# Selecting the rows of B with all 128 rows of the array instead of 64, in a fused state-space, attention and mixture kernel

## What is computed

```python
x = L0_attn_x
x = x + 0.5 * _L0_ffn_ref(_layernorm(x), w_gate, w_up, w_down)
x = x + _L0_attn_ref(_layernorm(x), ...)
x = x + 0.5 * _L0_ffn_ref(_layernorm(x), w_gate, w_up, w_down)
x = x + 0.5 * _L1_ffn_ref(_layernorm(x), Wg, bg, W1, b1, W2, b2)
x = x + _L1_attn_ref(_layernorm(x), Wq, Wk, Wv, Wo, rel, gamma, beta)
x = x + 0.5 * _L1_ffn_ref(_layernorm(x), Wg, bg, W1, b1, W2, b2)
```

```python
deltaA = jnp.exp(delta[..., None] * A)
deltaBx = delta[..., None] * Bm[:, :, None, :] * u[..., None]
h = dA * h + dBx
y = jnp.einsum('ben,n->be', h, c)
```

## Time and profile before

| what | value |
|---|---|
| median of three executions | 2872.73 us |
| time of the profiled execution | 2876.84 us |
| its span, first to last instruction | 2875.1 us |
| TensorE (PE) busy | 2733.4 us, 95% |
| weight loads (PEld) busy | 1895.2 us |
| VectorE (DVE) busy | 1946.4 us, 68% |
| ScalarE (ACT) busy | 1606.0 us, 56% |
| GpSimd (POOL) busy | 1371.3 us, 48% |
| mean granted clock of TensorE | 0.953 of 2.4 GHz |

### The profile page before, as it was taken

The page is one execution under the profiler, slowest core; times in us unless marked ns, Lnnn a source line. Parts: engine busy times, 40 slices in busy tenths (PEclk is TensorE's granted clock), DMA queues, the critical chain, the costliest instruction groups (busy, mean ns, idle before and its releaser), DMA issues.

```text
span 2875.1 us, 41563 instructions
## 1 busy us (share of the span) xinstructions
PE 2733.4 (95%) x14913; PEld 1895.2 (66%) x14913; DVE 1946.4 (68%) x3753; ACT 1606.0 (56%) x3405; POOL 1371.3 (48%) x1226
## 2 busy tenths in 40 slices
PE   7999999999999989999799899999999999999888
PEld 7777875786577655666366566656575666678675
DVE  5868887697868687676867886687858666432320
ACT  2433436435664556656486556756675676465654
POOL 2448475563737365454716474274636635311111
PEclk9999999999999989799799999999999999999899
DMA  4223122131213021211202121121202112000000
GB/s 147 67 67 104 55 64 74 45 92 42 79 40 96 23 73 39 70 49 49 77 20 78 37 76 31 49 70 31 75 19 86 36 52 67 1 4 1 1 5 4
DMA packets 88573, 150.60 MB, mean 52 GB/s; under 512 B 10565, under 2 KB 21485, under 8 KB 88110
## 3 DMA queue, kind: packets, MB, share of 16 engines
q1 hardware_dynamic: 88366, 147.94, 16.4%
HBM read 145.26 MB, written 2.65 MB: 51 GB/s over the span
## 4 chain that ended last, share of the span: by engine, by line
PE 83%; ACT 7%; DVE 5%; POOL 3%; issue 2%; DMA 0%; POOLq 0%; SPq 0%; ACTq 0%; DVEq 0%
PE c_bank L912 16%; PE c_bank L920 16%; PE c_bank L1338 13%; PE a_bank L758 8%; PE a_bank L748 5%; PE b_bank L1072 3%; PE b_bank L1061 3%; PE a_bank L727 2%; PE b_bank L1085 2%; PE b_bank L1084 2%; PE b_bank L582 1%; PE b_bank L563 1%; PE b_bank L565 1%; PE b_bank L1083 1%; PE a_bank L764 1%
## 5 line engine op out<-in xcount | busy, mean ns | idle before, releaser
L829 POOL TENSOR_TENSOR prod_c<-hst,prod_c 128x512 f32<-128x512 f32 x512 | 666.0, 1306 | 502.0 <-DVE hst L706 478.1
L706 DVE TENSOR_TENSOR_SCAN hst<-dA,a_bank 128x512 f32<-128x512 f32 x512 | 621.0, 1213 | 16.3 <-ACT dA L818 6.8
L912 PE MATMUL c_bank<-c_xT,w 128*128 128x512 f32 x1024 | 544.3, 638 | 7.7 <-ACT weighted_y L955 4.7
L818 ACT ACTIVATE dA<-delta,a_neg 128x510 f32<-128x510 f32 x512 | 364.2, 718 | 330.8 <-DVE hst L706 325.4
L920 PEld LDWEIGHTS c_bank<-w,hid 128*128 128x128 f32 x4096 | 491.2, 193 | 80.0 <-issue 47.5
L920 PE MATMUL c_bank<-w,hid 128*128 128x128 f32 x4096 | 529.4, 281 | 3.1 <-ACT hid L947 3.1
L1338 PEld LDWEIGHTS c_bank<-ident 128*128 128x128 f32 x3752 | 449.1, 193 | 66.4 <-issue 60.4
L1338 PE MATMUL c_bank<-ident 128*128 128x128 f32 x3752 | 483.4, 281 | 0.5 <-ACT weighted_y L955 0.4
L947 ACT ACTIVATE hid<-c_bank,b 128x512 f32<-128x512 f32 x512 | 349.7, 687 | 185.2 <-PE c_bank L912 183.5
L700 DVE TENSOR_TENSOR a_bank<-du,a_bank 128x512 f32<-128x512 f32 x512 | 350.5, 685 | 132.7 <-PE a_bank L748 128.5
L971 POOL TENSOR_TENSOR xs<-xs,weighted_y 128x512 f32<-128x512 f32 x128 | 167.9, 1312 | 544.6 <-ACT weighted_y L955 544.0
(11 more groups left out here) (179 smaller groups left out, 3550.8 us busy)
## 6 DMA issues: line engine op xcount, KB each, us to landing
prod_c<-c_rows SPq DMA_DIRECT2D x512, 256.0 KB, 3.1
w<-in_w SPq DMA_DIRECT2D x2, 2048.0 KB
xs<-in_x SPq DMA_DIRECT2D x8, 256.0 KB, 8.6
bias<-skew SPq DMA_DIRECT2D x1, 2048.0 KB, 8.8
out_dram<-xs SPq DMA_DIRECT2D x8, 256.0 KB, 2.3
in_wT<-in_in_wT SPq DMA_DIRECT2D x1, 512.0 KB
c_rows<-bcC SPq DMA_DIRECT2D x16, 32.0 KB, 1.6
b_hq<-in_w_gu SPq DMA_DIRECT2D x1, 384.0 KB, 3.2
```

The source lines that it names most:

```text
L706: nc.vector.tensor_tensor_scan(hst[:, s % RS, :], dA[:, s % RA, :], b_bank, 0.0, ALU.mult, ALU.add).then_inc(M.h.sem, 1)
L818: nc.scalar.activation(half_batches(dA[:, s % RA, :], 1), half_batches(delta[:, h, :], 1), ACT.Exp, scale=a_neg[:, l, h, n:n + 1]).then_in ...
L829: nc.gpsimd.tensor_tensor(prod[:, s % RP, :], hst[:, s % RS, :], cring[:, s % RC, :], ALU.mult).then_inc(M.pp.sem, 1)
L912: nc.tensor.matmul(S.bank[up_bank(e, c)][:, :], w1[:, e, c * 128:(c + 1) * 128], S.xT[:, :], start=True, stop=True).then_inc(M.up.sem, 1)
```

## The change

`bc3` is cleared as a whole at the start, `sel` is made over all 128 partitions (`eye2` has zero rows in partitions 0 to 63), and the B step reads all 128 rows of both, so zeros are multiplied by zeros in the lower half. The sum is the same. The clearing counts on the semaphore `s_const`, so the waits on it are one higher, and VectorE's first step that writes to `bcr`, ahead of the one that writes to `bc3`, waits for it too.

```diff
@@ mamba_dve
             dve.wait_ge(M.cE.sem, L.at(M.cE, 1))
+            if l == 0 and L.g == 0:
+                dve.wait_ge(s_const, 3 + RA)
@@ mamba_pe
-                    nc.tensor.matmul(S.bank[2 - s % 2 * 2][:, :], sel[64:128, s % NST, :], bc3[64:128, :],
+                    nc.tensor.matmul(S.bank[2 - s % 2 * 2][:, :], sel[:, s % NST, :], bc3[:, :],
                                      start=True, stop=True).then_inc(M.b.sem, 1)
@@ a_pe, and the same in a_act, b_pool and c_pool
-                        pe.wait_ge(s_const, 2 + RA)
+                        pe.wait_ge(s_const, 3 + RA)
@@ a_pool
-            pool.wait_ge(s_const, 1 + RA)
+            nc.gpsimd.memset(bc3[:, :], 0.0).then_inc(s_const, 1)
+            pool.wait_ge(s_const, 2 + RA)
             pool.wait_ge(s_wm, 16 * len(load_m))
-            nc.gpsimd.tensor_copy(sel[64:128, :, :], eye2[64:128, :].unsqueeze(2).to_broadcast([64, NST, 128])).then_inc(s_const, 1)
-            yield
-            pool.wait_ge(s_const, 2 + RA)
+            nc.gpsimd.tensor_copy(sel[:, :, :], eye2[:, :].unsqueeze(2).to_broadcast([128, NST, 128])).then_inc(s_const, 1)
+            yield
+            pool.wait_ge(s_const, 3 + RA)
```

The five step orders are made anew: the same steps of each lane in the same sequence, otherwise interleaved, and 1843 filler steps in the place of 1876. One line of each ORDER_PE, from the second pass:

```diff
-    "d10adb5aba2b4a2b2a3b2dad10a2d5ad9ad10a2d9a2d3ad7ad2a2d7ad3a2d7ad3a2d7ad3a2d12ad13ad7ad20ad4a3d13ad5ad3a2d7a"
...
+    "adb5a2bad2ad4b4ab4a3d7ad7ad2a2d7ad10a2d10a2d3ad7ad2a2d7ad2a2d7ad2a2d7ad3a2d12ad13ad7ad20ad3a3d13ad5ad3a2d7a"
```

More of the change, by code:

```diff
@@ new lines @@
+    "c4b2cbc12b3d2bdbcbcb4c3bc2bc2b2c2b2c4bcb2cb2c2b2cbcb3cbcb2cb2cb2cbcb2cbcbcbcbcb3cbcb2cbcb2cbcbcb2cb2cb2cbcbc"
+    "b2cbcbcb4cbcb3cb3cb3cb3cb3cb3cb3cb3cb3cb3cb2cb2cb2cbc2bc2bc5bcb3cbcbcbc2bcb2c4bc2bc2b2cbcb3cb3cb3cb3cb3cb3c"
+    "b3cb3cb3cb3cb3cb3cb3cb3cb2cb2cbcbcbcbcb3cbcbcb2cbcbcbcb2cb3cbcb2cbcb2cbcbcb2cb3cbcb2cbcb2c2bcbcb2cbcbcbcb2"
+    "d27c68")
+ORDER_DVE = (
+    "ab70aba7b8a3baba3ba3b5ab2ababa4baba6baba2ba2ba2ba2ba2ba2ba2ba2ba8ba2bab7a135b13a7ba3bab2abab2a3bababababa2b"
+    "a2ba5ba2ba2ba2ba2ba2ba2ba2ba2ba2ba8ba2ba2ba2ba2ba2ba2ca2ca2ba2bca2ba2ba2ba2ba2ba2ba2cacb5ababcbcbcbabcbcb5ab"
+    "a5b2a4b4a14ba72b13a7ba3bab2abab2a3bababababa2ba2ba5ba2ba2ba2ba2ba2ba2ba2ba2ba2ba8ba2ba2ba2ba2ba2ba2ca2ca2ba2"
+    "bca2ba2ba2ba2ba2ba2ba2cacb4abab2cbcbabcbcbcb5aba5b2a4b4a14baba2ba2ba2ba2ba7b5a8b2aba2ba2ba2bababa2ba2ba2ba2b"
+    "a2ba2ba2ba2ba2ba2ba2ba2babab2a2b2ab2a2b6a2b2a5bab9ab2a5b2a4b3abababa11baba2ba2ba2ba2ba2ba2ba2ba2ba2ba2ba2ba2"
+    "ba2ba2ba2ba2ba2ba2ba2ba2ba2ba2ba2ba2ba2ba2ba6ba2ba3b5cbc4a2b3ab5c4a2ca8ba6ba8baba2bab5aba2ba2ba2ba2bab5aba2b"
+    "ab2a4b5cbacac3b7aba7cbaba2ca2ba2ba2babcbcbaba2ba2ba2ba2ca2ba2ba2ba2ba2ba2bab4ababab2a4bab8a6ba4b5ab2ab2ab2a3"
+    "b3ababa2ba2ba2baba2ba2ba2ba2ba2ba2bab2a2b2a2b2a2b2a2b2a2b2a2b2a2b2a2b2a2b2ab2a2b2ab2a2b2a2b3aba2b2a2b2ab2a2"
+    "b2a2b2a2b2ab2a2b2a2b2ab2a2b2a2b2a2b2a2b2c4bcb2ab8cbc3a5ca2ba2b23a13b5abacaca2ca2babababababcbcba10b2a2bababa"
+    "bcababababababa2cababa2cababababcababababababa2ca3b5aba5b4aba5b8abab3aba3b4a2b18ab2a2b2a2baba3b2ab2ab2ab2ab2"
+    "a3baba3bababab2aba2b2a2b2a2baba2b2a2b2a2baba2b2a2b2a2b2a2b2a2b2a2b2a6baba4b5abaca2ca2cababcbabababababaca6ba"
+    "ba2babababcabcbcbcb2abacb2ab10a8b5abac4acbab3ababababa8baba3babababababababababa2baba2babababababababababa7"
+    "b5aba5b4aba8b8ab4abab4acab2aca2cb2ab2aca2b2ab2a2b2cb4a2b4a5b2ab19aba2b2a3b2a2b2a2b4ab2ab2ab2ab2a3b2a2b2ab2a7"
+    "baba4b5aba2ca2cbabababababababaca2ca2ca2baba2babababababababababa3baba3babababababababababcacacaca2b5abacaca"
+    "c2bcbcb5aba2b10ababa3baba3bab5ab2ababa8b5aba5b4aba8b8abab7abab2a2b2a2b2a2b2ababababa2b2a2b2acab2acacbcba2bab"
+    "acababa2baba3b2a5b2a3b2a4b2a2b2a3b2ab4ab2ab2a5b2ab12ab2a4b2a2b2a5b2a4b2abacabaca2bcabcaca5bababab4aba7cacbcb"
+    "ca3cbabababababababababa3baba2babababababababababa6b5aba2ca2cb4abaca2ca2ca3b9a2b3ab13ab2a3b2a2b2ab2aca2c3b2a"
+    "b2ab2ab2ca3b2ab2a3b2a2b2ab2a7b2a3b2a2b3aba3b2ab2a3b2a2b2a2b2a2b2a3b2a2b2a2b2a2b2a2baba2baba11ba2ba4ba2ca2ca2"
+    "cac2a3b5c4b7cb30cbc4b13cb3cbc2b5cb69c5b10c5b86c10")
@@ new lines @@
+ORDER_POOL = (
+    "ab5a2b2a13ba86bab2a18ba12ba15ba2ca2b2aca7ca6ca6ca9ca3ca9ca3ca6bab2a18ba12ba15ba2ca2b2aca6baca3ba3ba3ca3ca6c"
+    "a5ca5ca2ca61bcabca4ca2baca5ca2ca2ba2cbcac2aba16ba12cbacabab2c3a8ca14ca8ca18cbabcbc2bcacaba2ca4cacba2ca13ba10"
+    "ba5ba4baba3ca2ca2caca7ca17ca4ba3ca2ca3baca10bab3ca7ca3baca7ca3ba2ca4ba2cba3ba3cac2a15ca4ca3ba4ca4cba5ca8ca2b"
+    "aca3c2a6ba5ba3bacbcbcabaca2baba3ca4caca4c2a24ca7ca3c3a2baca4c3ba15cba6ca3caba3ca2ba4ba3ca3bacac3a7ca6ca8ca6c"
+    "a4ca12ca5c3ab2c2bc2bc2b2cbc11b3c17")
```

127 lines of the change are left out of this document (49 added, 78 removed).

## The result

| | before | after |
|---|---|---|
| median of four executions | 2874.28 us | 2762.74 us (2759.75 to 2769.06) |
| ratio of the times, 95% interval | | 0.9607 (0.9576 to 0.9639) |
| time of the profiled execution | 2876.84 us | 2769.06 us |
| its span | 2875.1 us | 2767.3 us |

The change makes the kernel 3.9% faster. The profiled executions are 107.8 us apart; 94 us were forecast. (The median of before stood at 2872.73 us when the forecast was made; the fourth execution, run beside the kernel after, is 2885.39 us.)

A forecast was written before the change was run, and what follows sets the result against it. TensorE, 95% busy, was taken as the bound, with VectorE and GpSimd close behind in four filler passes. B steps (135 us) and fillers (7) free 142 us; 94 arrive: 2783 us profiled, 2779 median, 8-in-10 range 2728 to 2835.

The forecast's parts named there:

- The price of a B step: On TensorE between 128-row matmuls: 0.10 us into it, 0.08 to 0.09 out, 0.11 for late weights; 0.29 us in all.
- the step that carried the forecast: The B step's delay comes from its changed row height, not its bf16 type, so 128 rows save the full 0.29 us.
- What reaches the end: Of 142 us freed on TensorE, 15 in passes 0, 1, 2 and 4 and 79 elsewhere shorten the total: 94 us.
- gains of 4, 3, 4 and 4 us: Passes 0, 1, 2 and 4, full of fillers, were to shorten this much: 15 of 43 us freed on TensorE.
- the bound of the scan step: In passes 0, 1, 2 and 4 a scan step needs 1.93 us on GpSimd and 1.91 on VectorE, against 2.1 now.
- a fifth: Taken off the 99 us freed in the other passes, for chain latencies and added fillers, leaving 79 us.
- Behind the last scan: The stretch with no B step left was to stay as it is, some 430 us, with 28 more fillers.
- The additions: Clearing bc3, at most 0.52 us on GpSimd, and sel over 128 partitions, 1.9 us as before, hidden before the first B step.
- The whole gain: Rival: the new interleaving fills every hole and all 142 us arrive, 2735 us, range 2715 to 2750; 13%.
- Half the gain: Rival: the data type costs something, 0.08 to 0.2 us saved per step, or VectorE bounds dense passes; 2800 to 2855; 17%.
- no gain: Rival: the delay comes with bf16 weights, so only the 7 us of fillers go, 2866 to 2873; 5%.
- The slower case: Rival: less busy TensorE in passes 0, 1, 2 and 4 gets the lower clock, 170 to 200 us longer, 2950; 5%.

The follow-up runs named there:

- the two heights in one kernel: The kernel after with every odd B step (256 of 512) reading only partitions 64 to 127: 2821.66 us, ratio 0.981.
- a third height: The kernel after with the B step reading only 32 rows, partitions 64 to 95, leaving out the third part of B: 2864.54 us, ratio 0.9936.
- the scores with fp32 data: The kernel after with attention scores made from all 128 rows of q and k instead of a head's 24, computation changed: 2709.21 us, ratio 0.9407.
- taking away 16 pairs of changes: The kernel after with the product of gate weights and experts' second biases reading 128 rows instead of 8: 2745.23 us, again 2748.44; ratios 0.9526 and 0.9538.

## Why the prediction was right

- **The price of a B step** (0.29 us) holds to about 0.01 us at each of its three places, as the timelines of the result show, and the step that carried the forecast, that it is the height and not the type, is shown three times: by the two heights in one kernel, by a third height with the same price, and by the scores with fp32 data. Nothing of the bound for a price of the data type remains. One reading under this step was weaker than it looked: L1061's q and k are typed fp32r and take one record for each product, where a product of L912 takes two (256 and 1024 records for 256 and 512 products), so that L1061 differed from L912 by more than its 24 rows. The experiment with the scores closes this, as it changes the height alone. And 41 B steps last over 0.55 us, so ran at the lower clock, where I had counted some 30; that is 1 us of the sum. Where the trace had spoken against the rule of the Trainium skill (TensorE: Matmul & The Clock Gate, Part 3, What overlaps and what doesn't) that weights are loaded ahead only in other row groups, it did so rightly: L913's weights are loaded under the B step, all 128 rows in both. The Trainium skill's other rule, on draining (TensorEngine Tiling (Array Packing), Key Properties), agrees with all of these traces.
- **What reaches the end.** 108 of the 142 us, 76%, where 94, 66%, were forecast. Both parts of the sum, 15 and 79, were a little low. In passes 0, 1, 2 and 4 I took gains of 4, 3, 4 and 4 us. The first and the last start of the scan in pass 1 and pass 2 tell 4.7 and 5.7 (line, engine, durations in ns, first and last start): before,

```profile
L706 DVE TENSOR_TENSOR_SCAN hst<-dA,a_bank x32: 1220/1220/1221, 216.3 to 282.2; 128x512 f32<-128x512 f32 x32
...
L706 DVE TENSOR_TENSOR_SCAN hst<-dA,a_bank x32: 1156/1207/1221, 327.2 to 412.9; 128x512 f32<-128x512 f32 x32
```

and after:

```profile
L707 DVE TENSOR_TENSOR_SCAN hst<-dA,a_bank x32: 1220/1221/1221, 211.1 to 272.3; 128x512 f32<-128x512 f32 x32
...
L707 DVE TENSOR_TENSOR_SCAN hst<-dA,a_bank x32: 1153/1207/1221, 316.3 to 396.3; 128x512 f32<-128x512 f32 x32
```

  The term mis-sized here is the bound of the scan step. I had added the durations on VectorE, 1.220 + 0.688 = 1.91 us, and had put GpSimd's 1.93 above it. In the timeline of the kernel after from 235 us on, a multiplication starts before the scan ahead of it has ended, and a step takes 1.84:

```profile
234.86 0.68 DVE L701 TENSOR_TENSOR a_bank<-du,a_bank 128x512 f32<-128x512 f32 x1
...
235.57 1.22 DVE L707 TENSOR_TENSOR_SCAN hst<-dA,a_bank 128x512 f32<-128x512 f32 x1
...
236.70 0.68 DVE L701 TENSOR_TENSOR a_bank<-du,a_bank 128x512 f32<-128x512 f32 x1
```

  Of the 31 distances between scan starts in this pass, 29 are 1.84 or 1.85; the two others, 3.53 and 4.12, hold other steps of VectorE. GpSimd is slower, 3.80 us for two steps in most of the pass, but it catches up in those two gaps, so it doesn't hold the scans back here.

  The other passes I had charged with a fifth. From the first scan start to the last of the whole kernel it was 2347.9 us and is 2237.5:

```profile
L706 DVE TENSOR_TENSOR_SCAN hst<-dA,a_bank x512: 1153/1217/1222, 97.1 to 2445.0; 128x512 f32<-128x512 f32 x171
```

```profile
L707 DVE TENSOR_TENSOR_SCAN hst<-dA,a_bank x512: 1153/1217/1222, 98.3 to 2335.8; 128x512 f32<-128x512 f32 x171
```

  110 us less; with about 21 of them in the four passes (5.3 and 5.5 in passes 0 and 4 by the same view), 89 us came through in the rest, where 79 of 99 were forecast. But part of these 89 is the new interleaving, for which my sum has no term. The kernel with the new height and the old orders shows the height by itself: 2253.8 us from the first scan start to the last, 94 less than before, of which 22 lie in the four passes and 72 in the rest. The height frees 135 - 37 = 98 us there (37 are the 128 B steps of the four passes), so 73% arrived, less than the four fifths that I took, and the new orders brought 17 us more. The two errors point in opposite ways. That the sum came so close is in this part luck.
- **Behind the last scan** 430 us were expected to stay: from the last scan start to the end of the span it is 430.1 us before and 431.5 after, with 28 more fillers in it. With the new height and the old orders it is 425.7.
- **The additions** cost next to nothing. The clearing of bc3 takes 524 ns, as taken from the earlier trace rows, and starts at 2.4 us. The first B step starts at 90.0 us (89.6 with the old orders) where it was 88.8. Whether this 1 us comes from the additions was not tested.
- **The rivals.** The whole gain (2735) didn't arrive, as VectorE bounds the filler passes. Half the gain and no gain fell with the type. The slower case fell as the clock stayed at 1.00 in passes 0 to 2. Its price, for passes full of fillers at the lower clock, was never put to the test. What the experiment without fillers shows is that then the lower clock costs a scan only about 1 us, since VectorE sets the pace.
- **The new interleaving**, which I gave no term of its own, is worth some 15 us with the new height and nothing without.
- **The signs.** The starts around the B step and the weights loaded under the matmul ahead of it came as forecast, and TensorE's busy time fell by 123 us. Two signs were wrong. In pass 1 it is VectorE and not GpSimd that has the least idle time (61.3 against 58.1 of 63 us), and TensorE shows gaps of under 1 us until a third of the fillers is taken out. And the passes with few fillers are not each 6 to 9 us shorter: from first to last scan start they change by between 20 us less (pass 15) and 20 us more (pass 7), as the new orders put other work into them. With the old orders eleven of the twelve are 5 to 10 us shorter, and pass 9 by 1 us.

## What to carry to other kernels

A matmul of 64, 32, 24 or 8 rows between matmuls of 128 costs more than its columns: here 0.29 us for each B step amid full-height ones. Where TensorE is the bound, about three quarters of it or a little more was felt in the total (73% with the old orders, 79% with half of the steps); in the four passes that VectorE bounds it was much less (with 32 rows they are 13 us longer, from first to last scan start, for 37 us more on TensorE). Zero rows cost nothing: at 128 rows the next start is 0.22 us behind the B step's. So a small contraction that stands alone between full ones is better padded with zeros to 128 rows than sliced. 65 and 96 rows needed no padding here. Look for the price in the distances between starts and in where the next weight load begins; the B step's own record doesn't show it, as it lasts 0.38 or 0.39 us at 32, 64 and 128 rows.

## What the runs showed of the hardware that I had not expected

The price of a change of height is the same from 64 and from 32 rows (0.10 us into it, 0.10 out of it, 0.11 for late weights), and from 65 and 96 rows there is none. And the clock's share can move with a small change: taking away 16 pairs of changes, worth 6.4 us by their rows, went with a mean clock of 0.966 or 0.967 in place of 0.955 to 0.957 and brought 13 to 17 us by the medians (2748.44 and 2745.23 against 2761.7 and 2762.74), in two runs of it.
